# Heads 4 and 5 of a seventh sample turned by DMA, and a new order around the second root and the weight loads

## The reference, cut to what matters

```python
q, k, v = x @ Wq.T, x @ Wk.T, x @ Wv.T           # 32 query heads, 8 key heads, D = 128, per sample
q, k = rope(rmsnorm(q, wq), pos), rope(rmsnorm(k, wk), pos)
k_all = concat([k_cache[block_table], k])        # 512 cached + 128 new keys = 640
v_all = concat([v_cache[block_table], v])
scores = where(valid, q @ k_all.T * D**-0.5, -1e30)
x = x + (softmax(scores) @ v_all) @ Wo.T
```

## Time and profile before

| what | us |
|---|---|
| median of three runs | 1277.1 |
| lowest and highest | 1275.13, 1280.2 |
| the profiled execution's own time | 1275.63 |
| its span in the profile | 1273.9 |
| TensorE busy | 1257.2 |
| VectorE busy | 913.3 |
| GpSimd busy | 826.7 |
| ScalarE busy | 785.6 |

### The profile page before, as it was taken

The page is one execution under the profiler, slowest core; times in us unless marked ns, Lnnn a source line. Parts: engine busy times, 40 slices in busy tenths (PEclk is TensorE's granted clock), DMA queues, the critical chain, the costliest instruction groups (busy, mean ns, idle before and its releaser), DMA issues.

```text
span 1273.9 us, 25215 instructions
## 1 busy us (share of the span) xinstructions
PE 1257.2 (99%) x6553; PEld 1076.1 (84%) x6553; DVE 913.3 (72%) x2658; ACT 785.6 (62%) x1850; POOL 826.7 (65%) x810
## 2 busy tenths in 40 slices
PE   9999999998999999999999999999999999999998
PEld 8888877877888888888888888888888888888886
DVE  6532357778877777887777788777777887777774
ACT  5731333637666668676666676766667767666664
POOL 2110011338778888687888887877887869788863
PEclk9999999999999999999999999999999999999999
DMA  8321224277667678755676787567777775667744
GB/s 290 115 83 38 84 71 142 60 262 211 126 132 160 148 142 228 189 130 129 145 157 153 157 223 193 128 136 146 161 159 201 170 199 128 135 155 151 156 101 83
DMA packets 356912, 190.41 MB, mean 149 GB/s; under 512 B 302402, under 2 KB 321218, under 8 KB 356546
## 3 DMA queue, kind: packets, MB, share of 16 engines
q1 hardware_dynamic: 337824, 136.32, 46.1%
q10 hardware_dynamic: 11410, 33.69, 8.1%
q0 software_dynamic: 7568, 19.14, 6.7%
HBM read 119.71 MB, written 16.91 MB: 107 GB/s over the span
## 4 chain that ended last, share of the span: by engine, by line
PE 86%; DVE 6%; issue 4%; DMA 3%; ACT 2%; ACTq 0%; POOL 0%; DVEq 0%; POOLq 0%
PE bank L1697 18%; PE tail L1737 14%; PE wide L1767 14%; PE tail L1804 13%; PE wide L464 4%; PE wide L544 3%; PE bank L1720 3%; PE wide L1731 3%; PE bank L464 3%; PE tail L464 3%; PE wide L599 2%; DMA spread<-one_over_denominators 1%; PE bank L544 1%; PE bank L599 1%; DVE tail L2270 1%
## 5 line engine op out<-in xcount | busy, mean ns | idle before, releaser
L1737 PE MATMUL tail<-prT,vt 128*128 128x512 f32 (+1 forms) x975 | 251.0, 400 | 0.2
L1737 PEld LDWEIGHTS tail<-prT,vt 128*128 128x128 f32 x975 | 173.1, 189 | 36.3 <-DVE prT L2221 5.2
L1804 PE MATMUL tail<-woT,oT 128*128 128x512 f32 x768 | 179.6, 390 | 0.9 <-DVE oT L2274 0.9
L1804 PEld LDWEIGHTS tail<-woT,oT 128*128 128x128 f32 x768 | 144.1, 188 | 31.1 <-DVE oT L2274 1.3
L1767 PE MATMUL wide<-kT,qT 128*128 128x320 f32 x512 | 159.4, 311 | 2.0 <-DVE mx L2250 1.7
L1767 PE MATMUL wide<-kT_low,qT 128*128 128x320 f32 x512 | 158.3, 309 | 0.0
L1767 PE MATMUL wide<-kT,qT_low 128*128 128x320 f32 x512 | 158.1, 309 | 0.0
L1354 POOL TENSOR_TENSOR tick<-tick 128x1 f32<-128x1 f32 x255 | 53.1, 208 | 154.9 <-DMA turned<-parts 47.1
L1993 ACT ACTIVATE raw<-raw,nm,q_scale 128x640 f32<-128x640 f32 x124 | 114.6, 925 | 61.1 <-DVE nm L2253 59.0
L1412 POOL TENSOR_TENSOR parts<-raw,parts 128x1280 f16<-128x1280 f32 x55 | 145.7, 2649 | 8.0
L2250 DVE CUSTOM_DVE_ANT_0 raw<-wide,bias 128x640 f32<-128x640 f32 x124 | 101.7, 820 | 27.4 <-issue 26.9
(11 more groups left out here) (308 smaller groups left out, 3040.2 us busy)
## 6 DMA issues: line engine op xcount, KB each, us to landing
w_ring<-pair_weights SPq DMA_DIRECT2D x80, 256.0 KB, 4.3
k_raw<-k_pages SPq DMA_DIRECT2D x512, 32.0 KB, 1.8
v_raw<-v_pages SPq DMA_DIRECT2D x512, 32.0 KB, 2.7
spread<-one_over_denominators ACTq DMA_DIRECT2D x32, 512.0 KB, 4.2
xTb<-x_transposed ACTq DMA_DIRECT2D x31, 512.0 KB, 3.9
rope<-rope_tables SPq DMA_DIRECT2D x31, 256.0 KB, 3.3
out<-y POOLq DMA_DIRECT2D x31, 256.0 KB, 4.3
w_raw<-w_gate_up SPq DMA_DIRECT2D x10, 512.0 KB, 3.5
```

The source lines that it names most:

```text
L1737: last = nc.tensor.matmul(tail[g][:, first * S:end * S], vt[v_part][:, j, g * D:(g + 1) * D], prT[p_part][:, first:end, j, :], start=(j == ...
L1804: last = nc.tensor.matmul(place[:, :], oT[:, g, o_part, (h % REP) * S:(h % REP + 1) * S], woT[w_part][:, h, :], start=(h == o_part == w_pa ...
```

## The change

`THIRDS` becomes samples 2 to 6, so turn 7 of each pair becomes one whose back unit has heads 4 and 5 turned by DMA, and turn 6 moves into the loop. SyncE issues the two new transposes in turn 7 of pairs 0 to 2 between the fifth and the sixth weight chunk, and in turn 0 it issues the four chunks 12 to 15 behind the value pages instead of ahead. In the late turns VectorE does the last two groups of the second root between masks 2 and 3, the second normalise behind mask 3 instead of mask 0, and ScalarE copies its result behind exponential 4 instead of 0. GpSimd's second halving waits for both normalises (the buffer it writes lies over the spread reciprocals). The wait on `c_free[1]` is for VectorE's own earlier subtraction.

```diff
@@ -1280,7 +1280,7 @@
     def unit(pair, b):
         return pair * B + b
 
-    THIRDS = range(2, 6)
+    THIRDS = range(2, 7)
 
     def has_third(b):
 
@@ -1316,7 +1316,6 @@
             turn(pair, 2, before(pair * B + 2), True, True, True, None, True, True)
             with eng.Fori(0, len(THIRDS) - 1) as last:
                 turn(pair, last + 3, before(last + (pair * B + 3)), True, True, True, None, True, True)
-            turn(pair, 6, before(pair * B + 6), True, True, True, None, True, True)
             more = pair + 1 < NPAIR
             turn(pair, B - 1, before(pair * B + B - 1), True, True, True, "next" if more else None, True, more)
         turn(NPAIR, 0, before(NPAIR * B), False, True, True, None, False, False)
@@ -1399,6 +1398,8 @@
         def halve(u, before, n, k, first_turn, rest_too):
 
             pool.wait_ge(s_exp, u * HP + HALF * (k + 1))
+            if k and not first_turn:
+                pool.wait_ge(s_norm, u * G)
             carry(n)
             src, dst = (raw0, parts0) if first_turn else (raw, parts)
             nc.gpsimd.tensor_copy(dst[k][:, 0], src[:, k * HALF:(k + 1) * HALF, :]).then_inc(s_half, 1)
@@ -1514,25 +1515,24 @@
             turn(0, 1, 6, None, 2, left=LEFT)
             BEGUN = 12
             LOOP = BEGUN + CARRIES + 1
-            SIXTH = LOOP + THIRD_CARRIES * (len(THIRDS) - 1)
-            SEVENTH = SIXTH + CARRIES + 1
+            SEVENTH = LOOP + THIRD_CARRIES * (len(THIRDS) - 1)
+            AFTER = SEVENTH + CARRIES + 1
 
             def middle(pair):
                 turn(pair, 2, pair * NCARRY + BEGUN, 0, 3)
                 with pool.Fori(0, len(THIRDS) - 1) as b:
                     turn(pair, b + 3, b * THIRD_CARRIES + (pair * NCARRY + LOOP), b + 1, b + 4)
-                turn(pair, 6, pair * NCARRY + SIXTH, 4, 7)
 
             with pool.Fori(0, NPAIR - 1) as pair:
                 middle(pair)
                 turn(pair, B - 1, pair * NCARRY + SEVENTH, B - 3, 0, "next")
-                turn(pair + 1, 0, pair * NCARRY + (SEVENTH + CARRIES), B - 2, 1)
-                turn(pair + 1, 1, pair * NCARRY + (SEVENTH + 2 * CARRIES), B - 1, 2, "out")
+                turn(pair + 1, 0, pair * NCARRY + AFTER, B - 2, 1)
+                turn(pair + 1, 1, pair * NCARRY + (AFTER + CARRIES), B - 1, 2, "out")
             pair = NPAIR - 1
             middle(pair)
             turn(pair, B - 1, pair * NCARRY + SEVENTH, B - 3, None)
 
-            n = pair * NCARRY + (SEVENTH + CARRIES)
+            n = pair * NCARRY + AFTER
             add_share(NPAIR * B - 2, B - 2, n)
             pool.wait_ge(s_out, 16 * (NPAIR * B - 1))
 
@@ -1629,17 +1629,20 @@
 
         KEYS_FIRST = 11
         VALUES_FIRST = 7
+        WEIGHTS_FIRST = 5
 
         def run():
             for pair in range(NPAIR - 1):
                 load_unit(7, pair, 2)
-                with sp.Fori(0, len(THIRDS)) as b:
+                with sp.Fori(0, len(THIRDS) - 1) as b:
                     load_unit(2, pair, b + 3)
                 pages = pages_of(6, pair, B - 1)
                 load_keys(pair, B - 1, pages)
                 load_rope(pair, B - 1)
                 turn_probs(pair, B - 2)
-                load_weights(pair + 1, 0, NRING)
+                load_weights(pair + 1, 0, WEIGHTS_FIRST)
+                turn_third(pair, B - 2)
+                load_weights(pair + 1, WEIGHTS_FIRST, NRING)
                 load_values(pair, B - 1, pages)
                 load_weights(pair + 1, NRING, 3 * KT)
                 pages = pages_of(3, pair, 0)
@@ -1647,9 +1650,8 @@
                 load_keys(pair + 1, 0, pages, 0, KEYS_FIRST)
                 turn_probs(pair, B - 1)
                 load_keys(pair + 1, 0, pages, KEYS_FIRST)
-                load_weights(pair + 1, 3 * KT, 4 * KT)
                 load_values(pair + 1, 0, pages)
-                load_weights(pair + 1, 4 * KT, NCHUNK)
+                load_weights(pair + 1, 3 * KT, NCHUNK)
                 pages = pages_of(4, pair, 1)
                 load_rope(pair + 1, 1)
                 load_keys(pair + 1, 1, pages, 0, KEYS_FIRST)
@@ -1659,7 +1661,6 @@
             load_unit(8, NPAIR - 1, 2)
             with sp.Fori(0, len(THIRDS)) as b:
                 load_unit(5, NPAIR - 1, b + 3)
-            load_unit(9, NPAIR - 1, B - 1)
             turn_probs(NPAIR - 1, B - 1)
             sp.wait_ge(s_wlo, chunks_done(NPAIR, 0))
             sp.wait_ge(s_out, 16 * (NPAIR - 1) * B)
@@ -2072,7 +2073,7 @@
                 if share or not front:
                     high_turned(u, before_back, 1, False)
                 if third and ahead:
-                    load_x(b + 1)
+                    load_x((b + 1) % B if isinstance(b, int) else b + 1)
             early(0)
             if share and not shares_first:
                 copy_share()
@@ -2112,7 +2113,7 @@
                     for i in late(extra, h, not back):
                         high_weights(chunk_pair(pair, extra), i)
                     exponential(h)
-                    if back and h == 0:
+                    if back and h == (REP if second_queries_late(pair, b, front, back) else 0):
                         copy_values(1)
                     if not back and h in (1, 3):
                         rest.token(h + 3)
@@ -2331,13 +2332,14 @@
             if front:
 
                 for h in range(HP):
+                    if late and h == 0:
+                        dve.wait_ge(c_free[1], before[1] + 3 + FIRST)
                     mask_max(h)
-                    if back and h == 0:
+                    if back and h == (3 if late else 0):
                         normalise(1)
-                    if late and h < 4:
-                        if h == 0:
-                            dve.wait_ge(c_free[1], before[1] + 3 + FIRST)
-                        next(second_root, None)
+                    if late:
+                        for _ in range((1, 1, 2)[h] if h < 3 else 0):
+                            next(second_root, None)
                     if back and h == (5 if late else 1):
                         low_values(0)
                     if back and h == (6 if late else 3):
```

## The result

The changed kernel takes 1291.8 us (median of 4 runs, 1286.32 to 1299.76), the kernel before beside it 1277.7: ratio 1.012, 95% interval 1.0065 to 1.0175. The forecast was 1273.6, so the sign was wrong, and the time lies above the stated range (1266.8 to 1279.0). The profiled execution took 1288.2 us (span 1286.5), which is 12.6 us more than the profiled one of before.

What follows compares the result with a forecast made beforehand. TensorE, busy 99% of the span, was taken as the bound. The terms +1.8 - 1.2 - 3.1 - 1.0 = -3.5 us, applied to the median 1277.1, gave 1273.6 us; the 8-in-10 range was 1266.8 to 1279.0.

Steps and rivals of the forecast that it cites:

- Part 1 in pairs 0 to 2: Sample 6's heads 4 and 5 by DMA in turn 7: TensorE's 1.2 us gain lost, +0.6 each, +1.8 us in all.
- The contention that I did price: GpSimd's added operations slowed by VectorE's SBUF reads: 0.6 us per pair if one is hit, within the costly end.
- My chain: GpSimd's added work delays VectorE's subtractions, masks 6 and 7, exponentials and ScalarE's casts by 1.6 to 1.75 us, then TensorE's sums.
- The idle time of 1.5 to 2 us ahead of turn 0's sums: Sign in pairs 0 to 2: TensorE idles before the next pair's turn 0 sums until ScalarE casts the turned probabilities.
- The second queue that I followed: SyncE issues the values 3.8 us later, ScalarE waits until 505.3 to 507.2; costly end +1.3 us per pair.
- Part 1 in the last pair: Sample 6's heads 4 and 5 by DMA in turn 7, without weight splits: additions hidden, full gain, -1.2 us.
- Part 2: Second root ahead of mask 3, second normalise behind it, in 4 turns: TensorE's 0.96 us q_scale wait goes; -3.1 us.
- Part 3: Four weight chunks behind the values at pair starts: the reciprocals' spread arrives in time; -1.0 us.
- a wait for ScalarE's squares: Sign in the reordered second-root turns: a wait for ScalarE's squares, shorter than the q_scale wait, takes its place.
- Rival B: ScalarE's copy in the dense stretch delays bank 0 by the full 0.96; sum -0.4, 1276.7 us; 12%.
- Rival A: Everything hidden: sample 6's DMA turning gives -4.8, with -3.8 and -1.0 the sum is -9.6, 1267.5 us; 30%.
- Rival C: Late values in pairs 0 to 2 slip ScalarE 3.8 us, TensorE 2.7 each; sum +2.8, 1279.9 us; 10%.

Runs made afterwards that it cites:

- e1: The changed kernel with VectorE's key mask issued ahead of GpSimd's six weight splits in turn 7 of pairs 0 to 2; 1278.7 us, ratio 1.0027.
- e3: The kernel before, with GpSimd's out<-y issue in turn 7 moved behind the split of the keys, directly ahead of the six weight splits; 1291.9 us, ratio 1.0112.
- e2: The changed kernel with one added wait of GpSimd for its own first split of the six; 1278.9 us, ratio 1.0027.
- e10: The changed kernel with GpSimd's out<-y issued behind the six weight splits of turn 7 instead of directly ahead; 1281.0 us, ratio 1.0033.
- e5: The kernel before with the second-root and normalise reorder and the four weight chunks behind the values, without sample 6's DMA turning; 1274.4 us, ratio 0.9979.
- e11: e1 with ScalarE's exponential 0 and values copy ahead of the values' cast in turn 7, each wq1T cast behind its exponential; 1279.6 us, ratio 1.0023.
- e7: The kernel of e5, plus sample 6's heads 4 and 5 turned by DMA in the last pair alone; 1272.7 us, ratio 0.9967.
- e4: The changed kernel with the key mask written as two operations, of 511 keys and of 1 key; 1285.2 us, ratio 1.0069.
- e9: The kernel of e3 with the key mask written as 511 keys and 1 key; 1293.5 us (one run).
- e13: The kernel of e3 with the key mask as 511 columns, output described as 7 rows of 73, plus one operation for the last key; 1293.9 us, ratio 1.0148.
- e12: e1 with SyncE's two new transposes behind three weight chunks instead of five; 1293.0 us, ratio 1.0117.

## Why the prediction was wrong, point by point

**Part 1 in pairs 0 to 2: +0.6 each forecast; in the changed kernel's turns 7 alone +6.61, +1.07, +7.14.** This is the step that failed. I counted what GpSimd and SyncE gain and lose in time, and put at nothing, without a word, the step that the branch moves: `add_share`, from ahead of the keys to directly ahead of six splits. In its place the runs show a VectorE operation of 0.48 us held for 7.46 and 8.41 us, which cost 12.2 us of the span (the changed kernel against e1). Nor did I ask what VectorE runs beside those splits. e3 shows that this one move makes the loss, e2 and e10 that it does so by the way the splits join. The contention that I did price, 0.6 us for a cast, is GpSimd held by VectorE, the other way round. This row of before was to be seen, the key mask in turn 7 of pair 1:

```profile
747.59 1.62 DVE L2257 TENSOR_SCALAR bias<-key_no,seq_f 128x512 f32<-128x512 int16 x1
```

It is three times its ordinary length in the same run of splits, and should have been the row to ask about.

With the mask out of the way the term is +1.6 us a pair (e1 against e5) instead of +0.6. My chain had its engine right, GpSimd: in turn 7 of pair 0 of e1 VectorE waits 0.27 and 1.29 us for its halves, and begins mask 6 at 517.04 instead of 514.97. It had its last link wrong. The idle time of 1.5 to 2 us ahead of turn 0's sums, which I named as the sign, did not appear: against the turn's start the sums begin 0.25 to 0.4 us later than in e5. Another 0.5 us come at the transposes of the rotated queries, where TensorE waits 0.33 to 0.36 us for VectorE's rotation (L2211), which stands behind masks 6 and 7. In pair 1 of the changed kernel there is also a wait of 0.28 us for wq1T's splits. The second queue that I followed, late values, is real, and their use at 506.26 lies within the forecast 505.3 to 507.2: TensorE waits 1.0 to 1.3 us a pair behind it in e1, but taking that away (e11) only uncovers GpSimd.

**Part 1 in the last pair: -1.2 forecast, -1.25 measured** (24.27 against 25.52), and -1.6 us between the medians of e7 and e5. This term was right.

**Part 2: -3.1, and Part 3: -1.0.** In turn 1 of pair 0 alone, where only Part 2 acts, the next output block begins at 335.35 instead of 336.0: -0.65, which is my 0.96 less 0.3. In part that is luck: TensorE reached the first wq0T matmul 1.34 us earlier (326.43 against 327.77), and gave back 0.7, of it 0.16 in a wait for a mask where I had none, and none in a wait for ScalarE's squares. At the starts of pairs 1 to 3 both act: -1.24, -0.44 and -0.64 (e5). With e5's own 0.74 in turn 1 that is -3.1 of the -4.1 forecast: the waits that these parts were to remove went, and the size is a quarter less. (In the prediction, half of the returned 0.3 in four turns gives 4 x 0.81 = -3.2, not -3.1; it changes nothing.) Rival B, the full return at bank 0, did not happen. The first normalise no longer waits for the spread in turn 0 of pair 1, where it waited 1.60 us:

```profile
539.24 0.70 DVE L2271 TENSOR_TENSOR tail<-tail,spread 128x512 f32<-128x512 f32 x1
```

**The sum.** By profiled executions: lock-out 12.2 (span of the changed kernel less that of e1), Part 1 otherwise 3 x 1.6 = 4.8, last pair -1.25, Parts 2 and 3 -3.1: +12.7, against 12.6 measured. The profiled execution of e1 is the fastest of its ten, and the changed kernel's median lies 3.6 us over its profiled one, so the terms hold for these executions and not for the medians. Rival A fell with the GpSimd chain. Rival C had the sign; it gave 1279.9. That this is close to e1 (1278.7), the kernel without the lock-out, is partly luck: the waits behind late values are 1.0 to 1.3 us a pair there, not the 2.7 that it was reckoned with.

What stays open: which property of the key mask makes it wait (e4, e9 and e13 did not separate it), why an issue of GpSimd directly ahead makes the splits join, and what slows all transfers in some turns 7.

## What to carry to other kernels

When a flag switches a branch, list every instruction that the branch places elsewhere, DMA issues too, and for each the engine beside it that shares a resource. Before adding to a dense run of GpSimd work, look in the trace for VectorE operations within SBUF whose longest duration is a multiple of their median; put such an operation a few microseconds ahead of the run, or break the run with a wait of GpSimd for itself, or issue GpSimd's DMA behind the run. An operation that was put ahead must also come in time: in e12 it fell back to the run. Take Part 1 only where there is no such run: in the last pair it gave its full 1.25 us.

## What of the hardware was unexpected

A VectorE operation of 0.48 us took up to 8.41 us beside back-to-back GpSimd operations, that is until the last of them ended. In these runs it was let in or not by what stood ahead of the run. Behind a DMA issue of GpSimd's queue the splits overlap by 0.25 to 0.35 us (1.5 to 1.6 us long, 1.25 apart), and the mask waited to their end, also when it had begun during the issue. Behind a cast, behind the subtraction of the keys, or behind a pause they are 1.29 us long and overlap by 0.04, and it got in, at a cost of about 0.2 us to one split (1.47 instead of 1.29).
